# Edge sum of a graph layer: the gathers' wait and the place of the rank table's matmuls

## The chip, the cores and the metric

The kernel runs on one core of one Trainium2 chip. The metric is the device time of one execution in microseconds, lower is better; shown is the median of several runs. The hardware profile is of one further execution.

## The reference

```python
xn = layernorm(x)                                  # x: (6250, 256) f32
edge = segment_sum(edge_weight[:, None] * xn[src], dst, 6250) + node_vec1
x = x + edge + linear_attention(xn)                # 4 heads, no softmax
z = layernorm(x)                                   # two of eight experts per row
x = x + sum_of_top2(softmax_weight * (relu(z @ W1 + b1) @ W2 + b2))
```

There are 200,000 edges, sorted by dst. The change concerns the segment sum alone.

## The kernel before, in words

The program is one sequence of stages: the layer norm and the attention's sums (front), the edge sum, edges left over (stragglers), routing, the experts. All engines run lists of instructions written out by hand, with semaphores between them; there is no scheduler.

**The edge sum** (edge_sum) holds acc, 49 tiles of 128 destination rows by 256 columns. The 49 source tiles are taken in NG = 7 groups of GRP = 7. For each group all 49 destination tiles are visited, in seven units of BU = 7 steps, so there are 49 units and 343 steps. The number of a step is t, its place in the unit is i (0 to 6), so "the third step" is i = 2 and "the last step" i = 6.

One step of a destination tile is, on the engines:
- VectorE makes 0/1 matrices: hots (L1284), hot_w with the edges' weights (L1288), and pick_w (L1295).
- TensorE multiplies them into four 128 x 128 blocks: blocks(t), 12 bf16 matmuls (L903). ScalarE copies these to SBUF (evacuate, L1027).
- TensorE multiplies the blocks by four source tiles that stay in SBUF (window), L911, and adds for three further source tiles the rows that GpSimd gathered by edge (picked), L915. Together these are rows(t): "the row products". Each f32 matmul shows as two.
- VectorE adds the result to acc: add(i), L1316. It signals o_added; the row products signal o_done.
- GpSimd issues three indirect DMAs of 128 rows (1 KB each) per step (L817) into one of SETS = 4 sets of buffers, set i % 4. A gather waits until the set's last user is done. Steps 0, 1 and 2 of a unit take over the sets of steps 4, 5 and 6 of the unit before, steps 3 to 6 those of 3 and, in this unit, 0 to 2. GpSimd issues in the order of the steps.

On TensorE the blocks are one step ahead: blocks(t + 1), then rows(t).

**Beside the steps** each of the first 42 units (more is true: all groups but the last) sorts one lot of edges, eight (AHEAD) lots before it is used. Its parts are spread over the unit's steps. On VectorE: two values (L1164) in step 0; in_row (L1125) and rank_ahead (L1134) in step 1; rank in step 2; values in steps 3 and 4; slots, 2 instructions of 128 x 2176, in step 5 (L1153); hot_tiles of the next lot (L1121) in step 6. In step 1 stands part (L1172, L1173) in four units of seven, or in step 3 make_list (L1180 to L1186) in the other three. On TensorE: base, 34 matmuls of 49 columns (L845), behind the row products of step 0; ScalarE takes it to base_sb (L989), which rank_ahead needs. And make_table, 34 matmuls of 196 columns (L854), which needs the values and the slots. It is the last work of a unit, and signals table_made. ScalarE unpacks the table in the next unit. VectorE's values wait for it too, since they overwrite its operands.

The order on VectorE at a unit's end is: step 5 hots and hot_w of the next step, add(4), slots; step 6 pick_w, hots, hot_w, add(5), hot_tiles; then add(6), which needs the row products of the last step; and then pick_w of the next unit.

The functions that carry this:

Of the kernel before, what the change touches and what calls it, by code (L numbers as in the profile page):

```python
# [33 lines left out]
CH = 34  # L34
STEP = 20
GRP = 7
REP = 16
SREP = 16
BU = 7
# [576 lines left out]
def edge_sum(nc, shared, edges, mixing, hot_w, xn_dram, xT_dram, base_dram, sum_dram, z_dram, Wg, bg, bias, wg, gb_row, G, NG, NT, N, D, HD):  # L616
# [14 lines left out]
    AHEAD = GRP + 1  # L631
# [7 lines left out]
    with ExitStack() as ctx:  # L639
        def sb(name, shape, dt=F32):  # L640
            return ctx.enter_context(nc.sbuf_tensor(name, shape, dt))
# [14 lines left out]
        slot = sb("slot", [P, CH, P], BF16)  # L656
        vals_all = sb("vals", [P, max(CH * FIELDS * NB, 2 * BU * D * 2)], BF16)
        vals = vals_all[:, 0:CH * FIELDS * NB].rearrange("p (c f b) -> p c f b", c=CH, f=FIELDS)
# [21 lines left out]
        def block_ps(par, j):  # L680

            return banks[par][:, j * P:(j + 1) * P]
# [3 lines left out]
        table_ps = banks[7][:, 0:FIELDS * NB].rearrange("p (f b) -> p f b", f=FIELDS)  # L686
# [39 lines left out]
        def later(s):  # L726

            return not (isinstance(s, int) and s == 0)
# [5 lines left out]
        def uses(i, u):  # L734

            return u * (2 if i % SETS < BU - SETS else 1) + i // SETS + 1
# [68 lines left out]
        @block.gpsimd  # L805
        def _(pool):
            pool.wait_ge(mix_added, (GRP - 1) * BU)
            for t in range(NG * NT):
                g, b = divmod(t, NT)
                i = t % BU  # L810
                if b == 0:
                    pool.wait_ge(listed, 3 * PICK * (g + 1))
                used = t - SETS if i >= SETS else t - BU + SETS if i < BU - SETS else t - BU
                if used >= 0:
                    pool.wait_ge(o_done, used + 3)
                for q in range(PICK):
                    pool.indirect_dma_start(out=picked[:, i % SETS * PICK + q, :], out_offset=None, in_=xn_dram,  # L817
                                            in_offset=bass.IndirectOffsetOnAxis(ap=place[g % 2][:, q, b:b + 1], axis=0)).then_inc(rows_in[i % SETS], 16)

        @block.tensor  # L820
        def _(pe):
# [4 lines left out]
            def turn_z(n):  # L826
                pe.wait_ge(z_done, n + 1)
                pe.wait_ge(zT_done, n + 2 if n <= LATE else n + 1)
                for k in range(2):
                    tr = pe.transpose(turn_ps(n)[:, k * P:(k + 1) * P], z[n // BU % 2][:, n % BU, k * P:(k + 1) * P], ident[:, :])  # L830
                tr.then_inc(z_turned, 1)

            def logits(n):
                pe.wait_ge(zT_done, n + 3)
                for k in range(2):
                    mm = pe.matmul(logit_ps[:, n * X:(n + 1) * X], zT[n % 2][:, k, :], wg[:, k, :], start=(k == 0), stop=(k == 1))
                mm.then_inc(logit, 1)

            def base(s):

                pe.wait_ge(tiles_done, s + 1)
                if later(s):
                    pe.wait_ge(base_in, s)
                for c in range(CH):
                    mm = pe.matmul(base_ps, before[:, :], hot_t[:, c, :], start=(c == 0), stop=(c == CH - 1))  # L845
                mm.then_inc(base_done, 1)

            def make_table(s):
                pe.wait_ge(vals_done, 3 * s + 3)
                pe.wait_ge(slot_done, s + 1)  # L850
                if later(s):
                    pe.wait_ge(unpacked, s)
                for c in range(CH):
                    mm = pe.matmul(table_ps, slot[:, c, :], vals[:, c, :, :], start=(c == 0), stop=(c == CH - 1))  # L854
                mm.then_inc(table_made, 1)

            def mix(t):
                c = t // BU
                if t % BU == 0:
                    pe.wait_ge(xT_in[c % 2], 16 * (c // 2 + 1))  # L860
                if t >= 4:
                    pe.wait_ge(mix_added, t - 3)
                for k in range(2):
                    mm = pe.matmul(mix_ps[t % 4], xT_part(t, k), M[:, k, :], start=(k == 0), stop=(k == 1))
                mm.then_inc(mixed, 1)
# [18 lines left out]
            def sort(s):  # L884
                if s == 0:
                    key_sums()
                base(s)
                if s == 0:
                    matrix()
                if later(s):  # L890
                    make_table(s - 1)
                    if s == 1:
                        pe.wait_ge(kv_step, 4)
                        pe.wait_ge(small_in, 3 * 16)
                    for i in range(BU):
                        mix((s - 1) * BU + i)

            def blocks(t, buf, pp):
                pe.wait_ge(w_done, t + 2)
                pe.wait_ge(a_copied, t + 1)  # L900
                for j in range(DENSE):
                    for part in range(3):
                        mm = pe.matmul(block_ps(pp, j), hot[buf][:, PICK + j, :], hot_w[buf][:, part, j, :],  # L903
                                       start=(part == 0), stop=(part == 2))
                mm.then_inc(a_done, 1)

            def rows(t, i, u, pp, par):
                pe.wait_ge(a_copied, t + 3)
                pe.wait_ge(o_added, t + 1)
                for j in range(DENSE):  # L910
                    pe.matmul(sum_ps[pp], block_sb[pp][:, j, :], window[par][:, j, :], start=(j == 0), stop=False)  # L911
                pe.wait_ge(pick_done, t + 2)
                pe.wait_ge(rows_in[i % SETS], 16 * PICK * uses(i, u))
                for q in range(PICK):
                    mm = pe.matmul(sum_ps[pp], pick_w[i % SETS][:, q, :], picked[:, i % SETS * PICK + q, :], start=False, stop=(q == PICK - 1))  # L915
                mm.then_inc(o_done, 1)

            def begin():
                make_table(AHEAD - 1)
                pe.wait_ge(mix_added, NT)  # L920
                blocks(0, 0, 0)

            def unit(g, k, odd, par, turn, more, after, q):
                t = g * NT + k * BU
                s = g * GRP + k + AHEAD
                pe.wait_ge(window_in[par], 16 * (turn + 1))
                for i in range(BU):
                    if i + 1 < BU:
                        blocks(t + i + 1, (i + 1) % 4, (odd + i + 1) % 2)
                    elif after:  # L930
                        blocks(t + BU, 0, 1 - odd)
                    rows(t + i, i, g * GRP + k, (odd + i) % 2, par)
                    if not more:
                        n = k * BU + i - BU - 1
                        if n >= 0:
                            turn_z(n)
                        if n >= 1:
                            logits(n - 1)
                    if more and i == 0:
                        base(s)  # L940
                    if more and i == 6:
                        make_table(s)

            def finish():
                for n in range(LATE, NT):
# [3 lines left out]
                pe.matmul(banks[3][:, 0:2 * X], ones_row[:, :], gb_row[:, :], start=True, stop=True)  # L949

            schedule(pe, sort, begin, unit, finish)

        @block.scalar
# [1162 lines left out]
```

## Time and profile before

| What | us |
|---|---|
| median of 3 runs without a profile | 2286.84 (2285.37 to 2287.73) |
| span of the profiled execution (its only time shown) | 2536.7 |
| TensorE busy in it | 2230.1 |
| VectorE busy | 1963.9 |
| GpSimd busy | 1551.1 |
| ScalarE busy | 1174.3 |
| edge sum, by TensorE's first and last blocks | about 302 to 2060 |

The profiled execution is 250 us longer than the runs. In all views times are from the start of the span. PE is TensorE's matmuls, PEld its weight loads, DVE VectorE, ACT ScalarE, POOL GpSimd. A matmul's end is modelled: where two groups follow each other, the start of the second is the better mark.

### The profile page before, as it was taken

The page shows a single profiled execution, that of the slowest core. Times are in us where ns is not written, and L with a number is a line of the kernel's source. Part 1 is how long each engine was busy: PE and PEld are TensorE (multiplying, and loading weights), DVE is VectorE, ACT ScalarE, POOL GpSimd, SP SyncE. Part 2 cuts the span into 40 slices and gives each one's busy share as a digit, 9 for nine tenths or more (in the row PEclk, how much of TensorE's full clock was granted, in tenths as well). Part 3 has the DMA queues.
Part 4 walks back from the last instruction along what each step waited for, and adds up shares of the span by engine and source line. Part 5 has one row for each costly group of instructions (what it writes and reads, how often), then busy time and mean ns, then how long its engine had stood idle before and what let it go on. Part 6 is the DMA issues. An engine that isn't in the chain of part 4 may idle for free. (4 is left out here: it accounts for less than half of the span.)

```text
span 2536.7 us, 45539 instructions
## 1 busy us (share of the span) xinstructions
PE 2230.1 (88%) x16549; PEld 1930.5 (76%) x16550; DVE 1963.9 (77%) x3350; ACT 1174.3 (46%) x1696; POOL 1551.1 (61%) x1356
## 2 busy tenths in 40 slices
PE   7987799999999899989988998999989944999993
PEld 4656687777887788778877787778877844999993
DVE  7989888788898788878877897879877757555552
ACT  2236544443444344434443454444322235888772
POOL 4750266666676566666665666666766612778883
PEclk9989999999999899989988999999999977999997
DMA  5532422222223222222222222222244453455555
GB/s 151 150 113 87 123 82 75 76 90 78 74 83 90 73 82 76 88 76 80 76 82 73 83 79 84 78 79 77 82 123 139 136 180 61 79 81 83 82 81 133
DMA packets 160931, 235.90 MB, mean 93 GB/s; under 512 B 54834, under 2 KB 121805, under 8 KB 160490
## 3 DMA queue, kind: packets, MB, share of 16 engines
q0 software_dynamic: 70896, 164.43, 25.4%
q1 hardware_dynamic: 75536, 55.29, 7.9%
q10 hardware_dynamic: 14314, 13.68, 1.6%
q8 instruction: 120, 1.97, 0.3%
q14 instruction: 65, 0.53, 0.1%
HBM read 186.46 MB, written 53.24 MB: 94 GB/s over the span
## 5 line engine op out<-in xcount | busy, mean ns | idle before, releaser
L817 POOL DMA_INDIRECT picked<-xn_dram,place x1029 | 1143.9, 1112 | 721.7 <-PE bank L915 289.8
L1027 ACT COPY stage<-bank 128x512 f32<-128x512 f32 x343 | 201.0, 586 | 796.9 <-remote 477.6
L915 PE MATMUL bank<-picked,pick_w 128*128 128x256 f32 x2058 | 518.4, 389 | 3.3 <-issue 3.3
L915 PEld LDWEIGHTS bank<-picked,pick_w 128*128 128x128 f32 x2058 | 405.7, 197 | 65.8 <-issue 5.2
L911 PE MATMUL bank<-window,stage 128*128 128x256 f32 x1568 | 416.9, 409 | 17.8 <-issue 12.8
L903 PE MATMUL bank<-hot_w,hots 128*128 128x128 bf16 x4116 | 312.0, 225 | 49.1 <-issue 44.8
L911 PEld LDWEIGHTS bank<-window,stage 128*128 128x128 f32 x1568 | 300.4, 202 | 65.1 <-issue 25.6
L1164 DVE TENSOR_TENSOR vals<-hot_t,field_rep 128x1666 bf16<-128x1666 bf16 x200 | 203.7, 1041 | 187.8 <-remote 180.2
L1288 DVE TENSOR_TENSOR hot_w<-hots,cur 128x1536 bf16<-128x1536 bf16 x343 | 328.6, 958 | 11.9
L903 PEld LDWEIGHTS bank<-hot_w,hots 128*128 128x128 bf16 x4116 | 267.1, 101 | 92.5 <-issue 54.5
L911 PE MATMUL bank<-stage 128*128 128x256 f32 x1176 | 315.5, 410 | 11.6 <-issue 10.4
L981 ACT COPY field_rep<-fields 128x1666 bf16<-128x1666 bf16 (+1 forms) x193 | 322.8, 1677 | 1.2 <-DVE vals L1164 1.2
L1284 DVE TENSOR_TENSOR hots<-ends,cur 128x1408 bf16<-128x1408 bf16 x343 | 303.1, 884 | 1.7 <-ACT cur L1021 1.7
L911 PEld LDWEIGHTS bank<-stage 128*128 128x128 f32 x1176 | 225.9, 203 | 49.0 <-issue 23.2
L1908 POOL DMA_INDIRECT sum_dram<-y,target x112 | 179.1, 1599 | 64.0 <-issue 31.1
L1316 DVE TENSOR_TENSOR acc<-acc,bank 128x256 f32<-128x256 f32 x343 | 142.3, 415 | 85.2 <-PE bank L915 44.7
L1295 DVE TENSOR_TENSOR pick_w<-hots,cur_w 128x384 f32<-128x384 bf16 x343 | 190.6, 556 | 0.2
L1899 POOL DMA_INDIRECT zin<-z_dram,token x112 | 115.5, 1031 | 83.4 <-POOLq L1600 49.6
L2002 PE MATMUL bank<-w,hh 128*128 x896 | 163.6, 282 | 1.1 <-DVE hl L2050 1.1
L854 PE MATMUL bank<-vals,slot 128*128 128x196 bf16 x1700 | 155.8, 249 | 4.9 <-issue 4.0
L854 PEld LDWEIGHTS bank<-vals,slot 128*128 128x128 bf16 x1700 | 147.9, 98 | 12.3 <-issue 5.8
L2002 PEld LDWEIGHTS bank<-w,hh 128*128 128x128 f32 x896 | 138.2, 189 | 1.4 <-issue 1.4
(253 smaller groups left out, 3414.6 us busy)
## 6 DMA issues: line engine op xcount, KB each, us to landing
picked<-xn_dram,place POOLq DMA_INDIRECT x1029
w<-in_L_ffn_W_dram SPq DMA_DIRECT2D x16, 512.0 KB, 8.9
xn_dram<-xn ACTq DMA_DIRECT2D x49, 128.0 KB, 1.9
xT_dram<-xT ACTq DMA_DIRECT2D x49, 128.0 KB, 2.1
base_dram<-acc SPq DMA_DIRECT2D x7, 896.0 KB
sum_dram<-acc SPq DMA_DIRECT2D x7, 896.0 KB
z_dram<-vals SPq DMA_DIRECT2D x7, 896.0 KB
out_dram<-sum_dram SPq DMA_DIRECT2D x1, 6250.0 KB, 21.8
```

Source lines behind the costliest of these rows:

```text
L817: pool.indirect_dma_start(out=picked[:, i % SETS * PICK + q, :], out_offset=None, in_=xn_dram, in_offset=bass.IndirectOffsetOnAxis(ap=plac ...
L854: mm = pe.matmul(table_ps, slot[:, c, :], vals[:, c, :, :], start=(c == 0), stop=(c == CH - 1))
L903: mm = pe.matmul(block_ps(pp, j), hot[buf][:, PICK + j, :], hot_w[buf][:, part, j, :], start=(part == 0), stop=(part == 2))
L911: pe.matmul(sum_ps[pp], block_sb[pp][:, j, :], window[par][:, j, :], start=(j == 0), stop=False)
L915: mm = pe.matmul(sum_ps[pp], pick_w[i % SETS][:, q, :], picked[:, i % SETS * PICK + q, :], start=False, stop=(q == PICK - 1))
L981: act.copy(field_rep[:, :, a:b, :], fields[:, a:b, bass.ds(s, 1), :].rearrange("p f a c -> p (a c) f").unsqueeze(3).broadcast_to([P, CH, b ...
L1027: act.copy(block_sb[pp].rearrange("p j c -> p (j c)"), banks[pp][:, :]).then_inc(a_copied, 1)
L1164: ins = dve.tensor_tensor(vals[:, :, f, :], hot_t[:, :, :], field_rep[:, :, f, :], ALU.mult)
L1284: dve.tensor_tensor(to[:, :, :].rearrange("p f (b r) -> p f b r", r=REP), ends[:, :, :].rearrange("p f (b r) -> p f b r", r=REP), of[:, i, ...
L1288: dve.tensor_tensor(hot_w[i % SETS][:, :, :, :].rearrange("p f g (b r) -> p f g b r", r=REP), to[:, AT_SRC:HOTS, :].rearrange("p g (b r) - ...
L1295: dve.tensor_tensor(pick_w[i % SETS][:, :, :].rearrange("p q (b r) -> p q b r", r=REP), hot[i % SETS][:, 0:PICK, :].rearrange("p q (b r) - ...
L2002: mm = pe.matmul(y_ps[i][:, n * D:(n + 1) * D], parts[a][:, c, n * P:(n + 1) * P], w, start=(m == 0), stop=(m == 3 * FC - 1))
```

## The change

The function make_table becomes begin_table (the three waits and the first 17 matmuls) and end_table (the other 17, and the signal). In each of the 42 units TensorE issues begin_table between the blocks and the row products of the last step, and end_table behind the row products. Where a table is made outside the units, the two halves stand together as before. On GpSimd the first gather of each unit's third step, from the second unit to the 43rd, waits also for table_made of the unit before.

```diff
--- before.py
+++ after.py
@@ -813,6 +813,8 @@
                 used = t - SETS if i >= SETS else t - BU + SETS if i < BU - SETS else t - BU
                 if used >= 0:
                     pool.wait_ge(o_done, used + 3)
+                if i == 2 and 0 < t // BU <= (NG - 1) * GRP:
+                    pool.wait_ge(table_made, AHEAD + t // BU)
                 for q in range(PICK):
                     pool.indirect_dma_start(out=picked[:, i % SETS * PICK + q, :], out_offset=None, in_=xn_dram,
                                             in_offset=bass.IndirectOffsetOnAxis(ap=place[g % 2][:, q, b:b + 1], axis=0)).then_inc(rows_in[i % SETS], 16)
@@ -845,14 +847,22 @@
                     mm = pe.matmul(base_ps, before[:, :], hot_t[:, c, :], start=(c == 0), stop=(c == CH - 1))
                 mm.then_inc(base_done, 1)
 
-            def make_table(s):
+            def begin_table(s):
                 pe.wait_ge(vals_done, 3 * s + 3)
                 pe.wait_ge(slot_done, s + 1)
                 if later(s):
                     pe.wait_ge(unpacked, s)
-                for c in range(CH):
-                    mm = pe.matmul(table_ps, slot[:, c, :], vals[:, c, :, :], start=(c == 0), stop=(c == CH - 1))
+                for c in range(CH // 2):
+                    pe.matmul(table_ps, slot[:, c, :], vals[:, c, :, :], start=(c == 0), stop=False)
+
+            def end_table(s):
+                for c in range(CH // 2, CH):
+                    mm = pe.matmul(table_ps, slot[:, c, :], vals[:, c, :, :], start=False, stop=(c == CH - 1))
                 mm.then_inc(table_made, 1)
+
+            def make_table(s):
+                begin_table(s)
+                end_table(s)
 
             def mix(t):
                 c = t // BU
@@ -929,6 +939,8 @@
                         blocks(t + i + 1, (i + 1) % 4, (odd + i + 1) % 2)
                     elif after:
                         blocks(t + BU, 0, 1 - odd)
+                    if more and i == 6:
+                        begin_table(s)
                     rows(t + i, i, g * GRP + k, (odd + i) % 2, par)
                     if not more:
                         n = k * BU + i - BU - 1
@@ -939,7 +951,7 @@
                     if more and i == 0:
                         base(s)
                     if more and i == 6:
-                        make_table(s)
+                        end_table(s)
 
             def finish():
                 for n in range(LATE, NT):
```

TensorE at the end of the first unit, before: the last blocks, the last row products (L911, L915), the table (L854), the next unit's blocks and rows.

```order
L903 MATMUL bank<-hot_w,hots 128x128 [waits a_copied,w_done]
L903 MATMUL bank<-hot_w,hots 128x128 x11
L911 MATMUL bank<-window,stage 128x256 [waits o_added,a_copied]
L911 MATMUL bank<-window,stage 128x256 x3
L915 MATMUL bank<-picked,pick_w 128x256 [waits rows_in2,pick_done]
L915 MATMUL bank<-picked,pick_w 128x256 x2
L854 MATMUL bank<-vals,slot 128x196 [waits unpacked,slot_done,vals_done]
L854 MATMUL bank<-vals,slot 128x196 x33
L903 MATMUL bank<-hot_w,hots 128x128 [waits a_copied,w_done,window_in0]
L903 MATMUL bank<-hot_w,hots 128x128 x11
```

And of the change, where those lines are L913, L921, L925, and the table is L856 and L860:

```order
L913 MATMUL bank<-hot_w,hots 128x128 [waits a_copied,w_done]
L913 MATMUL bank<-hot_w,hots 128x128 x11
L856 MATMUL bank<-vals,slot 128x196 [waits unpacked,slot_done,vals_done]
L856 MATMUL bank<-vals,slot 128x196 x16
L921 MATMUL bank<-window,stage 128x256 [waits o_added,a_copied]
L921 MATMUL bank<-window,stage 128x256 x3
L925 MATMUL bank<-picked,pick_w 128x256 [waits rows_in2,pick_done]
L925 MATMUL bank<-picked,pick_w 128x256 x2
L860 MATMUL bank<-vals,slot 128x196 x17
L913 MATMUL bank<-hot_w,hots 128x128 [waits a_copied,w_done,window_in0]
L913 MATMUL bank<-hot_w,hots 128x128 x11
L921 MATMUL bank<-window,stage 128x256 [waits o_added,a_copied]
L921 MATMUL bank<-window,stage 128x256 x3
```

The first table half and the wait for the slots and values now stand ahead of the row products of the last step, whose end signals o_done.

GpSimd from the first gather of a unit's second step on, before, two steps and the next:

```order
L817 DMA picked<-xn_dram,place 128x256 [waits o_done]
L817 DMA picked<-xn_dram,place 128x256 x2
L817 DMA picked<-xn_dram,place 128x256 [waits o_done]
L817 DMA picked<-xn_dram,place 128x256 x2
L817 DMA picked<-xn_dram,place 128x256 [waits o_done]
L817 DMA picked<-xn_dram,place 128x256 x2
L817 DMA picked<-xn_dram,place 128x256 [waits o_done]
```

And of the change:

```order
L819 DMA picked<-xn_dram,place 128x256 [waits o_done]
L819 DMA picked<-xn_dram,place 128x256 x2
L819 DMA picked<-xn_dram,place 128x256 [waits table_made,o_done]
L819 DMA picked<-xn_dram,place 128x256 x2
L819 DMA picked<-xn_dram,place 128x256 [waits o_done]
L819 DMA picked<-xn_dram,place 128x256 x2
L819 DMA picked<-xn_dram,place 128x256 [waits o_done]
```

The first gather of the third step has a second wait; the two gathers behind it and those of all later steps stand behind it.

## Rows read from the trace of the kernel before

**Rows 1.** Windows view, the edge sum: us, then PE, PEld, DVE, ACT, POOL busy (x count).
```profile
302.00:2060.00 1758.00, 1608.29 (x12054) 1392.28 (x12054) 1428.62 (x2169) 728.49 (x980) 1133.71 (x1021) 0.94 0.29 86
```

**Rows 2.** Timeline, TensorE: first and last table of the units (start, length, us).
```profile
337.96 3.06 PE L854 MATMUL bank<-vals,slot 128*128 128x196 bf16 x34
...
1806.90 3.06 PE L854 MATMUL bank<-vals,slot 128*128 128x196 bf16 x34
```

**Rows 3.** Timeline, VectorE and ScalarE in one pause; in brackets idle before.
```profile
1022.19 2.00 DVE L1164 TENSOR_TENSOR vals<-hot_t,field_rep 128x1666 bf16<-128x1666 bf16 x2 [3.79 <-remote]
...
1024.98 0.58 ACT L1027 COPY stage<-bank 128x512 f32<-128x512 f32 x1 [11.27 <-remote]
```

**Rows 4.** Timeline, TensorE: a base without a gap, and one undisturbed unit.
```profile
314.31 1.04 PE L845 MATMUL bank<-hot_t,before 128*128 128x49 bf16 x34
315.19 0.83 PE L903 MATMUL bank<-hot_w,hots 128*128 128x128 bf16 x12
...
731.62 3.06 PE L854 MATMUL bank<-vals,slot 128*128 128x196 bf16 x34
734.52 0.83 PE L903 MATMUL bank<-hot_w,hots 128*128 128x128 bf16 x12
...
738.26 1.16 PE L845 MATMUL bank<-hot_t,before 128*128 128x49 bf16 x34
...
740.57 1.95 PE L911 MATMUL bank<-stage 128*128 128x256 f32 x8
...
757.35 1.46 PE L915 MATMUL bank<-picked,pick_w 128*128 128x256 f32 x6
758.64 0.83 PE L903 MATMUL bank<-hot_w,hots 128*128 128x128 bf16 x12
759.31 1.95 PE L911 MATMUL bank<-stage 128*128 128x256 f32 x8
...
762.39 3.06 PE L854 MATMUL bank<-vals,slot 128*128 128x196 bf16 x34
```

**Rows 5.** Timeline, VectorE: the same unit.
```profile
733.19 0.42 DVE L1316 TENSOR_TENSOR acc<-acc,bank 128x256 f32<-128x256 f32 x1 [0.94 <-PE bank L915]
...
740.98 1.04 DVE L1134 TENSOR_TENSOR earlier<-hot_t,base_sb 128x1666 bf16<-128x1666 bf16 x1
...
749.52 0.27 DVE L1180 TENSOR_SCALAR table<-table 128x49 uint16<-128x49 uint16 x1
...
750.21 1.04 DVE L1164 TENSOR_TENSOR vals<-hot_t,field_rep 128x1666 bf16<-128x1666 bf16 x1
...
757.31 2.49 DVE L1153 TENSOR_TENSOR slot<-iota_j,rank_rep 128x2176 bf16<-128x2176 bf16 x2
...
763.30 0.41 DVE L1316 TENSOR_TENSOR acc<-acc,bank 128x256 f32<-128x256 f32 x1
```

**Rows 6.** Timeline, GpSimd: gathers of the same unit.
```profile
733.42 0.94 POOL L817 DMA_INDIRECT picked<-xn_dram,place  x1 [1.39 <-PE bank L915]
...
750.40 1.67 POOL L817 DMA_INDIRECT picked<-xn_dram,place  x1 [0.30 <-issue]
...
763.48 0.95 POOL L817 DMA_INDIRECT picked<-xn_dram,place  x1 [0.30 <-issue]
```

**Rows 7.** The page's group of the gathers, and a store with its landing (us).
```profile
L817 POOL DMA_INDIRECT picked<-xn_dram,place x1029 | 1143.9, 1112 | 721.7 <-PE bank L915 289.8
...
xn_dram<-xn ACTq DMA_DIRECT2D x49, 128.0 KB, 1.9
```

**Rows 8.** Timeline, ScalarE: the same unit.
```profile
759.57 0.58 ACT L1027 COPY stage<-bank 128x512 f32<-128x512 f32 x1 [1.41 <-PE bank L903]
```

**Rows 9.** Waits in 338 to 1806 us: total, times, longest.
```profile
DVE acc L1316 <- PE bank L915: 8.6, 11, 1.1
...
PE bank L915 <- issue: 2.9, 6, 1.0
```

## The prediction

> **What bounds the kernel now.** I read the page's busy times first, then the windows by stage, and then the timelines of single units of the edge sum, since an average over 2.5 ms hides what ends last. The change touches 42 of the 49 units of that stage.
>
> The edge sum runs from 302 to 2060 us, with TensorE busy for 1608 and VectorE for 1429 of its 1758 us [rows 1]. From the first to the last table of the unit loop (337.96 to 1806.90 us) lie 41 units, so one takes 1468.94/41 = 35.83 us [rows 2]. But the unit between the tables at 731.62 and 762.39 takes 30.77 us [rows 4], and one more near 1500 us is like it. All others hold pauses. In the one shown VectorE and ScalarE restart only at 1022.19 and 1024.98 us, after 3.79 and 11.27 us [rows 3], released by nothing of the kernel that the profile shows, and TensorE moves a few matmuls at a time.
>
> The profiled execution's own time is known by its span, 2536.7 us; the median of the runs is 2286.84. So 250 us exist in the profiled execution alone. If all of them lay in these 41 units, a real unit would be 35.83 - 250/41 = 29.7 us, less than TensorE's own work in it (below), so some lie elsewhere. I take the undisturbed unit for the real state and the pauses for a cost of recording. The sum therefore gives a difference per unit, and it is put on the median, not on the span.
>
> In the undisturbed unit three engines are full:
> - **TensorE**: a step (blocks and row products) takes 762.39 - 758.64 = 3.75 us, seven take 26.2. The table takes 734.52 - 731.62 = 2.90. The base sums take 740.57 - 738.26 less the blocks' 0.67 (759.31 - 758.64), which is 1.64; elsewhere they take 315.19 - 314.31 = 0.88 [rows 4]. Sum: 30.0 to 30.8 us.
> - **VectorE**: from the sum of the last step (the acc row at 733.19) to the same of the next unit (763.30) 30.11 us, without an idle moment [rows 5].
> - **GpSimd**: from the first gather of the third step (733.42) to that of the next unit (763.48) 21 gathers, 30.06 us [rows 6].
>
> So a unit without pauses takes 30.0 to 30.78 us. I take 30.4, the middle: with it the 41 units explain 41 x 5.43 = 223 of the 250 us and leave 27 for the rest of the program; 30.78 would leave 43, 30.0 only 11.
>
> **The change, part by part.**
> *The gathers' wait.* GpSimd now starts the third step's gathers behind the table and not behind the last step's row products, and all further gathers stand in order behind them. In the undisturbed unit that gather went off at 733.42. The table ends at 734.52, its signal takes about 0.26 us (below), and GpSimd starts 0.23 us behind VectorE when the same row products release both (733.42, 733.19). That gives 735.01, 1.6 us later. The closest customer is the sixth step: its gathers end at 750.40 + 1.67 = 752.07 and TensorE takes them at 757.35 [rows 4, 6]. Of these 5.3 us 3.7 stay for the transfer. No row times a gather's landing; the nearest is the store of a 128 KB tile, 1.9 us [rows 7]. GpSimd's own round is 30.06 + 0.23 = 30.3 us, inside the new unit below. Cost: nothing, hidden by the four sets of buffers; how that cover goes is rival 2.
>
> *The table in halves.* TensorE does the same 34 matmuls, so what counts is the order. Before, the row products of the last step stood ahead of the table. Now they stand behind 17 of its matmuls, and these wait for the slots (L1153). VectorE makes the slots in the sixth step and needs just those row products soon after, for its sum. That closes a ring from VectorE to TensorE and back, which every unit has to go round:
> 1. VectorE from the last step's sum to the end of the slots: 733.19 to 757.31 + 2.49 = 759.80, 26.61 us with no idle time [rows 5]. That unit has a make_list, five instructions in 0.69 us (749.52 to 750.21). Four units of seven have a part in its place, two instructions of that kind, by the same rate 0.28: 26.20. Mean (3 x 26.61 + 4 x 26.20)/7 = 26.38.
> 2. The signal to TensorE: I take 0.1, since TensorE already stands at this wait; no row has it, and 0.05 is the least I would believe.
> 3. Half the table: 2.90/2 = 1.45 [rows 4].
> 4. The row products of the step: 759.31 to 762.39, 3.08 [rows 4].
> 5. The signal back: ScalarE copies the blocks at 759.57, 0.26 us after TensorE's next group began at 759.31 [rows 4, 8]. I take 0.26. The lower bound is nothing. The sum at 763.30 did not wait and its row products' successor began at 762.39, so 0.91 is the upper one. (The sum at 733.19 had waited 0.94 us, to 1.57 behind its row products; with 763.30 beside it, I hold that for the end of a pause.)
>
> Sum 26.38 + 0.1 + 1.45 + 3.08 + 0.26 = **31.27 us** against 30.4. Before, parts 2 to 5 were not in VectorE's way: from the slots to that sum it took 763.30 - 759.80 = 3.50 us with its own work. Now they take 4.89 and it idles 1.39 us. TensorE idles too: it comes to the first half after its own 30.0 to 30.8 us and waits there 0.5 to 1.3.
>
> Nothing later takes this back, since the next round begins with the same sum. It is (31.27 - 30.4) x 42 = **36.5 us**, and 2286.84 + 36.5 = 2323. The bounds: with signals of 0.05 and 0 the ring is 30.96, against 30.78 that is 8 us (2294); with 0.91 it is 31.92, against 30.4 that is 64 us (2351).
>
> Another wait that moves stays covered: the base sums. VectorE uses them (through ScalarE) at 740.98, 7.79 us after its sum [rows 5], which is 8.1 us behind the row products; TensorE has them after 1.45 + 3.75 + at most 1.64 = 6.8, which leaves 1.2 for ScalarE. ScalarE and SyncE get no new wait. The sorting ahead of the loop and the last seven units issue the order of before.
>
> **A rule that speaks against the change.** A gather takes 0.94 us in the short cases and 1.67 in long ones, with 0.30 between two [rows 6]; the mean is 1.11 [rows 7]. The undisturbed unit had VectorE full, and its gathers still needed only 30.06 us, so the sum keeps the measured value. The Trainium skill, "SBUF — State Buffer", Who interferes with whom, says that a VectorE instruction with two SBUF inputs and a GpSimd instruction that reads SBUF exclude each other, and that the later one blocks entirely. The lengthened gathers agree with it, and by it gathers put to where VectorE has just restarted could all meet it, which is the far end of rival 2.
>
> **The rivals.**
> 1. *The ring has slack* (no difference). If a real unit already takes 31.3 us, for a reason the profile hides, the ring adds nothing: 2283 to 2291. Against it: the 41 units would explain 41 x (35.83 - 31.3) = 186 us, and 64 us of pauses would have to lie in the rest. Chance 0.09.
> 2. *GpSimd paces* (slower by more). Its round is now tied to the table: 0.23 us and 21 gathers. It decides from a mean of (31.27 - 0.23)/21 = 1.478 us on, the 0.30 included, against 30.06/21 = 1.431 measured. That is a margin of only 1 us a unit. At 1.50 a unit is 31.73 and the time 2287 + 1.33 x 42 = 2343. With every gather at 1.67 + 0.30 it would be 41.6 and the time 2757. Chance 0.09, nearly all at the near end.
> 3. *The half table covers a late gather* (faster). If, without the pauses, TensorE waits ahead of the last step's row products for their gathers, 17 matmuls that need no gather fill up to 1.45 us of that. It decides only if gathers land over 3.7 us after their issue and a real unit is above the ring; say it is 31.8 now and 0.5 goes: 2287 - 0.5 x 42 = 2266. Against it: TensorE's waits at L915 are 6 in 41 units, 2.9 us in all, and none is for a gather [rows 9]. Chance 0.07.
>
> **How the numbers follow.** The forecast, 2323 us, has 0.75. A measurement here can tell about 0.2% (4.6 us) from no change. Slower by more than that: forecast and rival 2, 0.84. Within: rival 1, 0.09. Faster: rival 3, 0.07. The bounds of the signals give 2294 to 2351, and I give 2293 to 2351: nearly all of the forecast and the near end of rival 2. Left out are rivals 1 and 3 and the far end of rival 2, just under 2 in 10.
>
> **What would show it.** In the new profile TensorE waits for the slots ahead of the first table half, 0.5 to 1.3 us, in many of the 42 units. VectorE's sum behind the hot tiles (L1121) waits for TensorE about 1.4 us; before, 41 units had 11 such waits, 8.6 us together [rows 9]. The third step's gather is released by the table. In a unit without pauses the pitch is 31.0 to 31.9 and VectorE's stretch from sum to slots stays 26.1 to 26.7. The prediction is wrong if undisturbed units keep 30.8, if TensorE waits at row products for gathers, or if VectorE reaches its sum after they are done.

## The result: 25.5 us slower

The changed kernel takes 2311.66 us (median of 4 runs, 2308.38 to 2313.89) against 2286.11 before (4 runs, 2279.40 to 2287.73): a ratio of 1.0119, 95% interval 1.0104 to 1.0133. The prediction had 2323 us with a range of 2293 to 2351, and slower at 0.84. Ratios here and below leave out runs more than 1.5% above the fastest of their kernel, so they can differ a little from the ratio of the medians.

The profile after holds none of the pauses of [rows 3]. Its span is 2308.7 us, and the run it was taken in has 2310.53, so only 1.8 us lie outside the span; these numbers show no cost of recording. From the page: busy time of the engines, and the groups of the gathers and of the sum, which was L1316 before (count, busy, mean ns, idle before, releaser).

```profile
PE 2100.5 (91%) x16549; PEld 1856.1 (80%) x16550; DVE 1955.4 (85%) x3350; ACT 1177.3 (51%) x1696; POOL 1582.3 (69%) x1356
...
L819 POOL DMA_INDIRECT picked<-xn_dram,place x1029 | 1173.7, 1141 | 469.8 <-issue 290.7
...
L1328 DVE TENSOR_TENSOR acc<-acc,bank 128x256 f32<-128x256 f32 x343 | 142.5, 415 | 88.4 <-PE bank L925 88.3
```

The timeline of TensorE, which answers to [rows 2]: the first halves of the first and the last of the 42 units.

```profile
331.39 1.61 PE L856 MATMUL bank<-vals,slot 128*128 128x196 bf16 x17 [1.52 <-issue]
...
1608.07 1.61 PE L856 MATMUL bank<-vals,slot 128*128 128x196 bf16 x17 [0.80 <-issue]
```

From the first to the last lie 41 units in 1276.68 us, 31.14 each, where the prediction had 31.27. They come in two lengths only, 30.93 us and 31.40. One whole unit on TensorE (answers to [rows 4]), of the shorter kind:

```profile
703.30 0.83 PE L913 MATMUL bank<-hot_w,hots 128*128 128x128 bf16 x12
705.39 1.61 PE L856 MATMUL bank<-vals,slot 128*128 128x196 bf16 x17 [1.26 <-issue]
706.84 1.92 PE L921 MATMUL bank<-stage 128*128 128x256 f32 x8
708.59 1.46 PE L925 MATMUL bank<-picked,pick_w 128*128 128x256 f32 x6
709.88 1.61 PE L860 MATMUL bank<-vals,slot 128*128 128x196 bf16 x17
711.33 0.83 PE L913 MATMUL bank<-hot_w,hots 128*128 128x128 bf16 x12
...
734.70 0.83 PE L913 MATMUL bank<-hot_w,hots 128*128 128x128 bf16 x12
736.33 1.61 PE L856 MATMUL bank<-vals,slot 128*128 128x196 bf16 x17 [0.80 <-issue]
```

The same unit on VectorE (answers to [rows 5]): the slots, the sum that closes the ring, and the next slots.

```profile
702.80 2.49 DVE L1165 TENSOR_TENSOR slot<-iota_j,rank_rep 128x2176 bf16<-128x2176 bf16 x2
...
707.84 1.04 DVE L1133 TENSOR_TENSOR hot_t<-iota_b,tile_rep 128x1666 bf16<-128x1666 bf16 x1
710.09 0.42 DVE L1328 TENSOR_TENSOR acc<-acc,bank 128x256 f32<-128x256 f32 x1 [1.21 <-PE bank L925]
...
733.74 2.48 DVE L1165 TENSOR_TENSOR slot<-iota_j,rank_rep 128x2176 bf16<-128x2176 bf16 x2
```

TensorE stands 1.26 us ahead of the first half at 705.39 and 0.80 at 736.33; between them lie 30.94 us. VectorE stands 1.21 us ahead of its sum at 710.09. No other wait of the two engines shows in the ring. The gather of the third step (answers to [rows 6]) is now released by the table's second half, and there GpSimd has idle time, 0.78 us beyond the usual 0.30:

```profile
710.22 0.95 POOL L819 DMA_INDIRECT picked<-xn_dram,place  x1 [0.30 <-issue]
712.25 1.34 POOL L819 DMA_INDIRECT picked<-xn_dram,place  x1 [1.08 <-PE bank L860]
713.89 1.60 POOL L819 DMA_INDIRECT picked<-xn_dram,place  x1 [0.30 <-issue]
```

### The profile page after: what moved, and what is told of

The parts are those of the page before. It is cut to its first block and busy times, and to the rows that moved or that the text cites. A ratio compares the mean times of both kernels' runs of the same rounds, so it can differ in the third digit from the quotient of the medians.

```text
span 2308.7 us, 45581 instructions
## 1 busy us (share of the span) xinstructions
PE 2100.5 (91%) x16549; PEld 1856.1 (80%) x16550; DVE 1955.4 (85%) x3350; ACT 1177.3 (51%) x1696; POOL 1582.3 (69%) x1356
## 5 line engine op out<-in xcount | busy, mean ns | idle before, releaser
L819 POOL DMA_INDIRECT picked<-xn_dram,place x1029 | 1173.7, 1141 | 469.8 <-issue 290.7
L925 PE MATMUL bank<-picked,pick_w 128*128 128x256 f32 x2058 | 500.3, 379 | 3.0 <-DMA picked<-xn_dram,place 3.0
L925 PEld LDWEIGHTS bank<-picked,pick_w 128*128 128x128 f32 x2058 | 390.8, 190 | 56.7 <-issue 3.5
L921 PE MATMUL bank<-window,stage 128*128 128x256 f32 x1568 | 380.8, 386 | 0.0
L921 PEld LDWEIGHTS bank<-window,stage 128*128 128x128 f32 x1568 | 282.6, 190 | 30.3
L913 PE MATMUL bank<-hot_w,hots 128*128 128x128 bf16 x4116 | 285.5, 219 | 4.3 <-DVE hot_w L1300 2.3
L921 PE MATMUL bank<-stage 128*128 128x256 f32 x1176 | 285.4, 385 | 0.0
L913 PEld LDWEIGHTS bank<-hot_w,hots 128*128 128x128 bf16 x4116 | 254.5, 98 | 36.9 <-DVE hot_w L1300 3.3
L921 PEld LDWEIGHTS bank<-stage 128*128 128x128 f32 x1176 | 211.9, 190 | 22.7
L1920 POOL DMA_INDIRECT sum_dram<-y,target x112 | 179.2, 1600 | 60.4 <-issue 30.2
L2003 PE MATMUL bank<-zh,w1h 128*128 128x256 f32 x448 | 132.9, 297 | 3.2 <-issue 1.9
L2003 PE MATMUL bank<-zh,w1l 128*128 128x256 f32 x448 | 127.9, 286 | 0.0
```

The source lines that it names most:

```text
L1920: pool.indirect_dma_start(out=sum_dram, out_offset=bass.IndirectOffsetOnAxis(ap=target[:, 2 * j + n:2 * j + n + 1], axis=0), in_=y[j % 2][ ...
L2003: mm = pe.matmul(hid_ps(i, c), ww[b][:, k * F + c * P:k * F + (c + 1) * P], zz[a][:, k, :], start=(m == 0), stop=(m == 5))
```

## The experiments

The pauses turned out to go with the chip. The twelve kernels ran in four groups, each on one chip with its own runs of the kernel before. In groups 1 and 4 (two chips) that kernel took 2525.71 and 2540.60 us and its traces held pauses. In groups 2 and 3 (two other chips) it took 2285.61 and 2286.78, and the traces of the edited kernels held none. By its times the result above belongs to the second kind. Times are compared inside a group only.

| Group | Kernel | median us | ratio to before, 95% |
|---|---|---|---|
| 1, pauses (before 2525.71) | e1 before | 2525.19 | 1.0016 (0.9979 to 1.0052) |
| | e2 halves only | 2435.75 | 0.9663 (0.9619 to 0.9706) |
| | e3 gathers' wait only | 2403.28 | 0.9543 (0.9506 to 0.9579) |
| | e4 no part ahead | 2501.33 | 0.9862 (0.9814 to 0.9910) |
| 2 (before 2285.61) | e5 changed kernel | 2309.33 | 1.0113 (1.0096 to 1.0130) |
| | e6 changed, in_row moved | 2308.95 | 1.0096 (1.0073 to 1.0120) |
| | e7 before, in_row moved | 2301.71 | 1.0081 (1.0064 to 1.0099) |
| | e8 before, two waits | 2288.79 | 1.0018 (1.0007 to 1.0029) |
| 3 (before 2286.78) | e9 halves only | 2312.38 | 1.0110 (1.0089 to 1.0132) |
| | e10 33 matmuls ahead | 2369.41 | 1.0359 (1.0340 to 1.0378) |
| 4, pauses (before 2540.60) | e11 gathers' wait only | 2464.60 | 0.9679 (0.9648 to 0.9710) |
| | e12 before | 2533.90 | 0.9976 (0.9940 to 1.0012) |

### Group 1: the parts alone, on a chip with pauses

**e1**, the kernel before, unchanged.

> The kernel before, unchanged, for a profile with fewer pauses. From the measured difference (25.5 us over 42 units, 0.61 each) and the mean unit of the changed kernel (31.13 us in its profile), a unit of the kernel before should take 30.52 us. Theory: 2286 us, and in stretches without pauses VectorE waits about 0.5 us a unit in places that the old profile hid. Rival (the pauses belong to the kernel before itself): its profile is over 2500 us long again.

**e2**, the halves without the gathers' wait:

```diff
--- changed kernel
+++ e2
-                if i == 2 and 0 < t // BU <= (NG - 1) * GRP:
-                    pool.wait_ge(table_made, AHEAD + t // BU)
```

> The changed kernel without the gathers' wait for the table. Theory (the ring through slots, half table, row products and sum sets the unit): as the changed kernel, 2311 us within 3, unit 31.13 us. Rival (GpSimd's wait makes the loss): back to 2286 us within 3.

**e3**, the gathers' wait without the halves: all 34 matmuls of the table behind the row products, in the order of before.

```diff
--- before
+++ e3
+                if i == 2 and 0 < t // BU <= (NG - 1) * GRP:
+                    pool.wait_ge(table_made, AHEAD + t // BU)
```

> The kernel before with the gathers' wait alone, the table whole and behind the row products. Theory: no difference, 2286 us within 3, since the gathers start up to 3 us later and have over 3 us to spare. Rival (GpSimd paces): slower by 10 us or more, with TensorE waits for gathers.

**e4**, the three waits ahead of the last row products and all 34 matmuls behind them, without the gathers' wait:

```diff
--- changed kernel
+++ e4
+    FIRST = 0
-                for c in range(CH // 2):
+                for c in range(FIRST):
-                for c in range(CH // 2, CH):
-                    mm = pe.matmul(table_ps, slot[:, c, :], vals[:, c, :, :], start=False, stop=(c == CH - 1))
+                for c in range(FIRST, CH):
+                    mm = pe.matmul(table_ps, slot[:, c, :], vals[:, c, :, :], start=(c == 0), stop=(c == CH - 1))
-                if i == 2 and 0 < t // BU <= (NG - 1) * GRP:
-                    pool.wait_ge(table_made, AHEAD + t // BU)
```

> No gather wait, and begin_table only waits (for values, slots, unpacking) ahead of the last row products; all 34 matmuls stand behind them. The ring keeps the wait and loses 17 matmuls: 31.13 - 1.45 = 29.7 us, below the 30.5 of the kernel before. Theory (the matmuls' length in the ring costs): 2286 us within 5. Rival (the wait for slots in that place costs by itself): 2295 us or more.

Measured: e1 is long again, as its rival said, in all its runs. e2 is 90 us faster than before and e3 122 us, where e2 was meant to be 25 us slower and e3 equal. e4 is 24 us faster by the medians, where it was meant to be equal. What the edits changed there was above all the pauses. Waits between 340 and 1800 us (total, times, longest), first of e1, then of e2 (L999 and L1174 are the lines of L989 and L1164):

```profile
ACT stage L1027 <- remote: 425.8, 44, 12.4
DVE vals L1164 <- remote: 164.8, 33, 8.2
ACT base_sb L989 <- remote: 83.2, 24, 7.8
```

```profile
ACT stage L1037 <- remote: 207.0, 22, 13.2
...
ACT base_sb L999 <- remote: 63.5, 27, 4.3
...
DVE vals L1174 <- remote: 36.3, 14, 3.9
```

These waits of ScalarE and VectorE, released by nothing that the trace shows, fell from 674 to 307 us. (In e3 the same three come to 256 us, in e4 to 669; e4's trace is of its longest run, 2521.13 us.) The ring is there in e2 as well, in the timelines of VectorE and TensorE:

```profile
739.02 0.42 DVE L1326 TENSOR_TENSOR acc<-acc,bank 128x256 f32<-128x256 f32 x1 [1.21 <-PE bank L923]
```

```profile
734.33 1.61 PE L854 MATMUL bank<-vals,slot 128*128 128x196 bf16 x17 [1.44 <-issue]
```

Here it costs less than the pauses that went. So this group can't judge the prediction, and why e2 and e3 have fewer pauses stays open. e4's question, whether the wait for the slots in that place costs by itself, was not put to a chip without pauses.

### Group 2: the ring cut at another place

**e5**, the changed kernel, unchanged.

> The changed kernel, unchanged. On the chip of the four runs so far the kernel before takes 2525 us and TensorE's signals of a finished table come 4.7 us late (median); where the changed kernel was profiled before they never came late. Theory A (the pauses are late signals from TensorE, set off where gathers are issued beneath the table's and base's dense matmuls; the wait and the halves both thin that out): on a chip with pauses 2330 to 2400 us against 2525 of the kernel before, on a chip without them 2311 against 2286. Theory B (only the ring matters): slower than the kernel before on any chip.

**e6**, the changed kernel with VectorE's in_row of the next lot moved from a unit's second step to behind hot_tiles, ahead of the sum that waits:

```diff
--- changed kernel
+++ e6
-                        in_row(s)
+                        if isinstance(u, int) and u == 0:
+                            in_row(s)
...
                         hot_tiles(s + 1)
+                        in_row(s + 1)
```

> The changed kernel with in_row (0.69 us) taken from VectorE's stretch between the last step's sum and the slots to behind the hot tiles, where VectorE idles 1.20 us. Ring theory: the ring falls from 31.13 to 30.44 us a unit, 29 us less than the changed kernel on either kind of chip if pauses stay the same, so about 2283 where the kernel before takes 2286. Rival (something else than the ring holds the unit at 31.13): no change from the changed kernel.

**e7**, the kernel before with the same move.

> The kernel before with the same move of in_row. Ring theory: there is no ring in the kernel before and VectorE's work stays the same, so no difference over 0.3% on a chip without pauses. Rival (VectorE waits for the base sums ahead of rank_ahead and in_row covers that): slower by up to 0.5 us a unit, 20 us.

**e8**, the kernel before with the gathers' wait for the table, and a second wait, for the base sums, ahead of the fifth step's:

```diff
--- before
+++ e8
+                if i == 2 and 0 < t // BU <= (NG - 1) * GRP:
+                    pool.wait_ge(table_made, AHEAD + t // BU)
+                if i == 4 and t // BU < (NG - 1) * GRP:
+                    pool.wait_ge(base_done, AHEAD + t // BU + 1)
```

> The kernel before with the gathers' wait for the table and one more: the fifth step's gathers wait for the unit's base sums. On a chip with pauses theory A expects fewer pauses under the base than with the first wait alone (2403 us against 2525), so below 2403; if the pauses under the base are not of the gathers' making, 2400 to 2410. On a chip without pauses 2286 to 2295, since the fifth step's gathers start about 1 us later and have 3.7 to spare.

Measured: e5 repeats the result, 23.7 us slower by the medians. e8 costs 3.2 us for the gathers' wait and a second one together; its interval (1.6 to 6.6) excludes zero, but more than half of it lies below the 4.6 us that the prediction asked of a difference. e6 should have won 29 us over e5 and won nothing. e7 lost 16 us by the medians, 18.5 by the ratio. Theory A of e5 and e8, that gathers issued beneath the table's and the base's matmuls set off the pauses, was not tested: this chip had none. Theory B of e5, slower on any chip, does not fit e2, which has the ring and was faster.

e6's trace shows what took the ring's place. (It is of the longest of e6's four runs, 2315.27 us; the shortest took 2301.03.) Waits between 390 and 1400 us, of the changed kernel and then of e6 (about 32 units each):

```profile
DVE acc L1328 <- PE bank L925: 39.7, 33, 1.2
PEld bank L856 <- issue: 37.5, 33, 1.4
POOL picked L819 <- PE bank L860: 35.6, 33, 1.1
PE bank L856 <- issue: 32.8, 33, 1.3
```

```profile
DVE acc L1328 <- PE bank L925: 37.9, 34, 2.8
...
PE bank L925 <- DMA picked<-xn_dram,place: 18.4, 34, 1.4
...
POOL picked L819 <- PE bank L860: 2.1, 7, 0.3
...
PE bank L856 <- issue: 0.2, 1, 0.2
```

The ring did open: TensorE's wait ahead of the first half fell from 32.8 to 0.2 us. In its place TensorE waits at the row products for gathers (L925 for the DMA), and GpSimd no longer waits for the table beyond its usual 0.30 us (35.6 to 2.1 us, 7 times 0.3). VectorE's sum still waits 37.9 us in all, but TensorE now comes to the table late, and no longer waits for the slots. That is rival 2's mechanism, in a kernel where I had not looked for it. The windows view of the gathers alone from 500 to 1400 us (length, busy and count, clock, DMA share, GB/s), for e6, e7, e8 and the changed kernel:

```profile
500.00:1400.00 900.00, 715.07 (x608) 1.00 0.31 93
```
```profile
500.00:1400.00 900.00, 714.15 (x611) 1.00 0.31 93
```
```profile
500.00:1400.00 900.00, 710.49 (x623) 1.00 0.32 95
```
```profile
500.00:1400.00 900.00, 692.65 (x608) 1.00 0.32 93
```

The mean gather is 1.176, 1.169, 1.140 and 1.139 us. With 0.30 between two, 21 of them fill 31.0, 30.8 and 30.2 us in e6, e7 and e8, and that is within 0.1 us the length of a unit there (900 x 21/608 = 31.1, by 611 it is 30.9, by 623 30.3). TensorE waits for gathers in all three. So GpSimd paces e6 and e7, and is full in e8 too. In the changed kernel the gathers fill 30.2 of 31.1 us, so it does not pace there. e7's recorded rival, VectorE waiting for the base sums ahead of rank_ahead, shows only 12 waits of about 0.2 us, 2.7 together, too little for its loss.

The mean depends on where in VectorE's work a gather starts. In the changed kernel, timelines of VectorE and GpSimd:

```profile
712.69 1.99 DVE L1176 TENSOR_TENSOR vals<-hot_t,field_rep 128x1666 bf16<-128x1666 bf16 x2
...
716.86 0.41 DVE L1328 TENSOR_TENSOR acc<-acc,bank 128x256 f32<-128x256 f32 x1
```
```profile
713.89 1.60 POOL L819 DMA_INDIRECT picked<-xn_dram,place  x1 [0.30 <-issue]
...
717.07 0.95 POOL L819 DMA_INDIRECT picked<-xn_dram,place  x1 [0.30 <-issue]
```

The gather that starts inside the values (two inputs in SBUF, the on-chip memory) takes 1.60 us, the one inside the sum, one of whose inputs lies in PSUM, where TensorE writes its results, 0.95. (The Trainium skill, "SBUF — State Buffer", Who interferes with whom, says that a VectorE instruction with two SBUF inputs and a GpSimd instruction that reads SBUF exclude each other; these rows agree.) Moving in_row moves both engines' work against each other. That this is what made e7's gathers longer is read from e8, the nearest kernel without the move; the kernel before has no trace without pauses to compare with.

### Group 3: the halves alone, and the dose

**e9**, the same kernel as e2.

> The table in halves around the row products of the last step, without the gathers' wait: the same kernel as e2_halves_only, for a chip whose traces hold no pauses. Theory (the ring paces, and the halves alone close it): the 42 units take 31.40 and 30.93 us as in the changed kernel, VectorE waits 1.2 us behind the hot tiles in each, and the time is that of the changed kernel, 2305 to 2314 us. Rival A (the ring costs nothing, the gathers' wait costs the 25 us): 2281 to 2290. Rival B (GpSimd, freed from the wait, drifts into VectorE's work and paces, as in e6): units of 31 to 33 us of changing length, 2312 to 2330 us. On a chip with pauses: 2436 us against 2525, as before.

**e10**, e9 with another number of matmuls ahead:

```diff
--- e9
+++ e10
+    FIRST = 33
-                for c in range(CH // 2):
+                for c in range(FIRST):
-                for c in range(CH // 2, CH):
-                    mm = pe.matmul(table_ps, slot[:, c, :], vals[:, c, :, :], start=False, stop=(c == CH - 1))
+                for c in range(FIRST, CH):
+                    mm = pe.matmul(table_ps, slot[:, c, :], vals[:, c, :, :], start=(c == 0), stop=(c == CH - 1))
```

> As e9, but 33 of the table's 34 matmuls stand ahead of the last step's row products and one behind them. Theory (ring): 16 more matmuls of 0.085 us each lie in the ring from VectorE's slots to its sum, so each unit takes 1.36 us more, 32.3 to 32.8 us instead of 30.93 and 31.40, VectorE waits 2.56 us behind the hot tiles, and the time is 42 x 1.36 = 57 us above e9, 2362 to 2372 us. Rival (TensorE's idle time is made up elsewhere, or the wait for the slots sets the cost and not the length of the part ahead): within 10 us of e9. On a chip with pauses the difference between the two is not defined by the theory; it should still be 30 to 57 us.

Measured: e9 takes 25.6 us more than before, the whole change's 25.5. So the halves alone carry the cost. Its units have the lengths of the changed kernel, 31.40 and 30.93 us, and VectorE and TensorE have the same waits between 390 and 1400 us:

```profile
DVE acc L1326 <- PE bank L923: 39.7, 33, 1.2
...
PE bank L854 <- issue: 32.8, 33, 1.3
```

Its gathers fill 31.0 of 31.1 us, so GpSimd is nearly full there too, yet TensorE has no wait for a gather in this stretch. e10 takes 57.0 us more than e9, and 57 was the forecast. Timelines of e10, VectorE and TensorE:

```profile
653.84 2.49 DVE L1164 TENSOR_TENSOR slot<-iota_j,rank_rep 128x2176 bf16<-128x2176 bf16 x2
...
662.49 0.42 DVE L1327 TENSOR_TENSOR acc<-acc,bank 128x256 f32<-128x256 f32 x1 [2.56 <-PE bank L924]
...
686.15 2.49 DVE L1164 TENSOR_TENSOR slot<-iota_j,rank_rep 128x2176 bf16<-128x2176 bf16 x2
```
```profile
656.43 2.97 PE L855 MATMUL bank<-vals,slot 128*128 128x196 bf16 x33 [1.74 <-issue]
```

VectorE waits 2.56 us instead of 1.21, 1.35 more for sixteen more matmuls (forecast 1.36), and this unit takes 32.31 us (653.84 to 686.15) instead of 30.94.

### Group 4: two more looks

**e11**, the same kernel as e3.

> The gathers' wait for the table alone, the table in one piece: the same kernel as e3_gather_wait_only, for a chip whose traces hold no pauses. Theory (the ring of the halves is the whole cost, the wait is free): the time is that of the kernel before, 2279 to 2291 us, TensorE has no wait at the table, and the units lie between TensorE's own 30.0 and some 31.5 us. Rival (the wait ties GpSimd to the table, and the 21 gathers behind it land late): TensorE waits for gathers more than in the kernel before, 2295 to 2312 us. On a chip with pauses: 2403 us against 2525, as before.

**e12**, the kernel before, for a trace of it without pauses.

> The kernel before unchanged, for a trace of it without pauses. Theory: its units are not all alike; those in which TensorE waits for nothing take its own 30.0 us, the others up to 31.5 us because gathers land late, and 42 of them take 25 us less together than in the changed kernel, so 30.5 us in the mean (31.13 less 0.6). Rival (VectorE's own work already paces it): every unit lies within 0.1 us of 30.1 or of 30.5 without a wait of TensorE for gathers. Time 2280 to 2290 us; with pauses 2505 to 2565.

Measured: the group fell on a chip with pauses, so neither answered its question: no trace of the unchanged kernel without pauses exists here, and the gathers' wait alone has no time without them; e8, which holds it and one more, bounds it. e11 gave 0.9679 where the same kernel as e3 gave 0.9543: the intervals don't meet, so on these chips an interval from one of them says little of the next.

## Why the prediction was right, point by point

**The ring** is the mechanism. It is seen in the trace after, it comes with the halves alone (e9), and its cost follows its length (e10, 57.0 us for 57). Shortening it (e6) removes TensorE's wait in it. Its terms, for a unit with a part, beside [rows 4, 5]:

| Term | forecast us | measured us |
|---|---|---|
| VectorE from sum to the end of the slots, with a part | 26.20 | 26.13 (710.09 to 736.22) |
| signal to TensorE | 0.10 | 0.11 (736.22 to 736.33) |
| half table | 1.45 | 1.45 (705.39 to 706.84) |
| row products | 3.08 | 3.04 (706.84 to 709.88) |
| signal back | 0.26 | 0.21 (709.88 to 710.09) |

For this unit the sum is 30.94 against a forecast of 31.09, and for the mean of all units 31.14 against 31.27. Every term was within 0.07 us. The signs named beforehand came: TensorE waits 0.80 or 1.26 us ahead of the first half in each unit (after the first), VectorE 1.2 ahead of its sum, and the gather is released by the table. Only the pitch of the shorter units, 30.93, lies just under the 31.0 to 31.9 that was named.

**The unit before** is the term that was mis-sized, beside the 0.13 of the ring. I took 30.4 us. The measured 25.5 us in 42 units are 0.61 each, which puts it at 31.14 - 0.61 = 30.53, if all of them lie in these units. By that, of the 11 us between forecast and result 5.5 come from each of the two. No trace shows the unit before directly. The nearest is e8, 0.2% from before: its tables run from 332.38 to 1582.73 us, 30.50 us a unit. So the middle of 30.0 and 30.78 came close by luck: it stood for no mechanism. In e8 the units are not alike. Its timeline of TensorE, first a unit in which it waits for nothing, then one with late gathers (the second table of each pair is cut short by the end of the stretch asked for):

```profile
944.09 3.06 PE L858 MATMUL bank<-vals,slot 128*128 128x196 bf16 x34
...
974.10 2.12 PE L858 MATMUL bank<-vals,slot 128*128 128x196 bf16 x23
```
```profile
456.01 3.06 PE L858 MATMUL bank<-vals,slot 128*128 128x196 bf16 x34
...
477.65 1.53 PE L919 MATMUL bank<-picked,pick_w 128*128 128x256 f32 x6 [0.26 <-DMA picked<-xn_dram,place]
...
482.02 1.53 PE L919 MATMUL bank<-picked,pick_w 128*128 128x256 f32 x6 [0.39 <-DMA picked<-xn_dram,place]
...
487.45 2.72 PE L858 MATMUL bank<-vals,slot 128*128 128x196 bf16 x30
```

They take 30.01 and 31.44 us. The first is TensorE's own work, and the changed kernel has the same: in the unit from 705.39 to 736.33, 30.94 less the wait of 736.33 - 734.70 - 0.67 (the blocks) = 0.96 us leaves 29.98. That the kernel before has both kinds of unit too is likely and not shown. e7, which has no wait of the gathers for the table, has TensorE waiting for gathers as well.

**"I take the undisturbed unit for the real state and the pauses for a cost of recording."** The first half held. The second was wrong, and it is the one step of the working that did not hold, though the number survived it: the runs of the kernel before on two chips take 2525 and 2541 us, as long as their traces, and the changed kernel's run and trace agree to 1.8 us. So the 250 us between the profiled execution and the runs are most likely the difference of two chips; which chip the profile came from is not on record. The difference per unit could be put on the median because the median, and the runs of the changed kernel, came from a chip without pauses. That was luck. Where the pauses occur the sign turns for the halves alone (e2), and no step of the working would have told that. The changed kernel itself was not run there.

**The gathers' wait.** Its cost, "nothing, hidden by the four sets of buffers", holds in the changed kernel: with e9 beside the result, 25.6 and 25.5 us, it adds nothing that can be told. Where the table stays whole, e8 puts it and a second wait together at 1.6 to 6.6 us. The trace after shows 1.34 and 1.60 us for the two gathers behind the wait, so two met VectorE's work, but over a unit the gathers come to less than in e9, whose gathers start at once (713.53 us for 607 from 500 to 1400 us, against 692.65 for 608).

**The rivals.** Rival 1 (slack) needed a unit before of 31.3 and it was 30.53. Rival 3 (cover for late gathers) was half there: in e8 and e7 TensorE does wait for gathers without the pauses, as in the unit of 477.65 above, and in the changed kernel these waits are gone (the page has 3.0 us before L925 in all, against 15.9 in e8). Two things can have taken them away: GpSimd has more time in the longer unit, or the half table and the wait ahead of it cover them. No run parts the two, but the place fits the cover: of e8's 19 such waits between its first and last table of the units, 14 stand ahead of the last step's row products, just where the first half now is, with 8.9 of the 10.3 us. Either way a unit of 30.53 is under the ring, so nothing is won. Rival 2 (GpSimd paces) did not decide, but its threshold did well in another kernel: it said 1.478 us for a gather with its gap, and e6, at 1.476, stood just there and came out as long as the ring, 31.1 us.

## What to carry to other kernels

When a piece of work on one engine is moved ahead of another, look for the engine that feeds the first and consumes the second: its path from the one to the other becomes a ring that every round must pass, and its length, summed from single rows, is the new lower bound of the round. Shortening a ring wins only down to the next pace, so weigh each nearly full engine first (here, in us a unit, TensorE 30.0, GpSimd 30.2 to 31.0, the ring 31.1). And where the profiled execution is a tenth longer than the runs, ask for another chip before trusting either the length or the sign of a difference.

## What was not expected of the hardware

Of the four groups' chips two ran the kernel before in 2286 to 2287 us (medians) and two in 2526 to 2541; none of its single runs lies between 2293 and 2505. In the traces with pauses TensorE issues a few matmuls at a time for some microseconds; here in e1:

```profile
734.19 1.02 PE L845 MATMUL bank<-hot_t,before 128*128 128x49 bf16 x22
735.71 0.18 PE L845 MATMUL bank<-hot_t,before 128*128 128x49 bf16 x1 [0.49 <-issue]
736.42 0.27 PE L845 MATMUL bank<-hot_t,before 128*128 128x49 bf16 x4 [0.53 <-issue]
```

The granted clock is 0.934 over e1's span against 0.971 in the changed kernel's. In this pause it fell behind the gaps and not ahead of them: it is still 1.00 from 735.70 to 738.00 us, where TensorE is busy for 0.83 of 2.30 us, and about half (0.50, the lower of its two levels, 1.2 GHz) from 738 to 744. So a pause costs its gaps and then some microseconds at half speed. A mean clock lower by 4% does not account for a time longer by 10%, so the gaps and waits hold more than half of it. What makes the pauses was not found.

A gather's issue on GpSimd takes 0.94 to 1.68 us in the changed kernel, by where it starts in VectorE's work, and there the two behind the wait have the same lengths in the next unit (1.34 and 1.60). A move that changes nothing in the amount of work (in_row, e7) came with a loss of 16 us, and with the wait the gathers are shorter on the mean than without it (1.139 us in the changed kernel, 1.176 in e9).
